# Distance-kernel attention on one core: heads in pairs, strips in two parts, rows read back in two steps

## The reference, cut to what matters

```python
qh, kh, vh = (q @ Wq), (q @ Wk), (q @ Wv)      # each as 16 heads of 8 features
dist = max(q_norm - 2*qk + k_norm, 0)          # per head, 512 x 512
scores = exp(-gamma[h] * SCALE * dist)
scores = where(triu(ones, k=1), scores, 0)
out = (scores @ vh) as (B, S, 128) @ Wo
x = x + out                                    # the input q is layernorm(x)
```

## Time and profile before

| | |
|---|---|
| median of three runs | 2600.57 us |
| the profiled execution, its own time | 2601.68 us |
| its span, first to last instruction | 2599.8 us |
| stage of the change, to the last value matmuls | 0 to 662 us |
| mean granted TensorE clock | 0.879 of 2.4 GHz |

### The profile page before, as it was taken

The page is one execution under the profiler, slowest core; times in us unless marked ns, Lnnn a source line. Parts: engine busy times, 40 slices in busy tenths (PEclk is TensorE's granted clock), DMA queues, the critical chain, the costliest instruction groups (busy, mean ns, idle before and its releaser), DMA issues. The chain is left out here.

```text
span 2599.8 us, 68776 instructions
## 1 busy us (share of the span) xinstructions
PE 2110.7 (81%) x27953; PEld 1528.7 (59%) x27953; DVE 1728.9 (67%) x3790; ACT 1376.9 (53%) x3916; POOL 678.4 (26%) x746
## 2 busy tenths in 40 slices
PE   3787878778689999999839945557999999993896
PEld 1444544444657677777627734455777777762775
DVE  6777787776537777777766676652777777777553
ACT  2666666656257777777613320014777777771332
POOL 4111111110123444444300003311444434431100
PEclk7888898887679999999969967766999999996998
DMA  5323332231000000000000000000000000000002
GB/s 164 108 85 89 95 107 82 88 99 54 1 9 18 19 18 19 19 11 19 19 1 1 2 1 1 0 1 9 19 11 18 19 18 19 19 19 1 1 1 66
DMA packets 65548, 87.64 MB, mean 34 GB/s; under 512 B 6849, under 2 KB 58946, under 8 KB 61766
## 3 DMA queue, kind: packets, MB, share of 16 engines
q1 hardware_dynamic: 64082, 82.81, 11.5%
q10 hardware_dynamic: 1152, 0.43, 0.1%
HBM read 35.42 MB, written 31.03 MB: 26 GB/s over the span
## 5 line engine op out<-in xcount | busy, mean ns | idle before, releaser
L392 ACT ACTIVATE r_pr<-r_dist,k_negc 128x1280 f32<-128x1280 f32 x256 | 333.3, 1330 | 157.6 <-PE r_dist L279 154.9
L1024 POOL TENSOR_TENSOR f2l_pn<-f2l_p,f2l_rs 128x512 f32<-128x512 f32 (+1 forms) x256 | 206.4, 828 | 343.5 <-DVE f2l_rs L951 343.5
L1024 POOL TENSOR_TENSOR f1l_pn<-f1l_p,f1l_rs 128x512 f32<-128x512 f32 (+1 forms) x256 | 206.4, 828 | 343.2 <-DVE f1l_rs L951 343.2
L470 DVE TENSOR_SCALAR r_pr<-r_pr,k_hi,k_lo 128x768 f32<-128x768 f32 x256 | 182.1, 711 | 123.1 <-ACT r_pr L392 123.0
L277 PE MATMUL r_dist<-r_qs,r_ks 54*128 54x384 bf16 (+2 forms) x768 | 165.3, 306 | 103.8 <-DMA r_ks<-rbf_rows 83.1
L474 DVE SCALAR_TENSOR_TENSOR r_pr<-r_pr,k_lo,r_cap 128x512 f32<-128x512 f32 x256 | 225.4, 880 | 0.0
L292 PE MATMUL r_acc<-r_pr,r_vp 128*32 128x128 f32 (+2 forms) x3584 | 195.1, 362 | 31.6 <-ACT r_ot L361 29.7
L901 ACT ACTIVATE f2l_p<-f2l_sm,f2l_nb 128x192 f32<-128x192 f32 x512 | 210.5, 423 | 1.3 <-DVE f2l_nb L944 1.3
L901 ACT ACTIVATE f1l_p<-f1l_sm,f1l_nb 128x192 f32<-128x192 f32 x512 | 210.4, 423 | 1.3 <-DVE f1l_nb L944 1.3
L277 PEld LDWEIGHTS r_dist<-r_qs,r_ks 54*128 54x128 bf16 x768 | 74.6, 103 | 205.5 <-DMA r_ks<-rbf_rows 87.5
L944 DVE TENSOR_REDUCE f1l_nb<-f1l_sm 128x4 f32<-128x768 f32 x128 | 121.8, 952 | 78.0 <-PE f1l_sm L793 77.9
(11 more groups left out here) (415 smaller groups left out, 5364.5 us busy)
## 6 DMA issues: line engine op xcount, KB each, us to landing
rbf_rows<-r_part SPq DMA_DIRECT2D x112, 128.0 KB, 1.8
r_qs<-rbf_rows SPq DMA_DIRECT2D x32, 432.0 KB
r_ks<-rbf_rows SPq DMA_DIRECT2D x32, 432.0 KB
f1l_vs<-f1l_vv SPq DMA_DIRECT2D x32, 256.0 KB, 3.9
f2l_vs<-f2l_vv SPq DMA_DIRECT2D x32, 256.0 KB, 3.9
rbf_rows<-r_part SPq DMA_DIRECT2D x16, 384.0 KB, 2.6
rbf_rows<-r_part SPq DMA_DIRECT2D x16, 256.0 KB, 2.9
out<-k_x SPq DMA_DIRECT2D x4, 1024.0 KB, 9.3
```

The costliest lines, as they stand in the source:

```text
L392: nc.scalar.activation(pr[:, u // 4 % 2, u % 4, :], dist[:, u % 2, 0:RCOLS], ACT.Exp, scale=K["negc"][:, h:h + 1]).then_inc(s_ex, 1)
L470: nc.vector.tensor_scalar(off, off, hi, lo, ALU.min, ALU.max)
L1024: ins = nc.gpsimd.tensor_tensor(pn[:, u % 2, at:at + HU * w].rearrange("p (k c) -> p k c", k=HU), p[:, u % 2, :, cols], r.broadcast_to([P, ...
```

## The change

- **Pairs.** The main loop goes over 8 pairs of heads instead of 16 heads. The matmuls of the two heads of a pair alternate, one in rows 0 to 53 of the array, the other in rows 64 to 117.
- **Two parts.** The diagonal blocks (512 columns) and the others (768 columns) are separate steps on every engine: `diagonal` and `others` on TensorE, two exponentials per head on ScalarE, `masked` and `bounded` on VectorE. Each has semaphores of its own.
- **Values.** Those of a quad are cut into four pieces of 384, 384, 256 and 256 columns, two per pair, and follow three pairs behind. `pr` becomes a ring of five pairs instead of two quads.
- **Projections.** The five uses stand after pairs 0, 1, 2, 3 and 5, `output` after pair 4, the norm of batch b+2 after pair 6. The norms go to 128 partitions of 256 columns by four matmuls in four column groups.
- **Rows in two steps.** SyncE reads the 48 main rows back as soon as they are written, before it waits for the norms; then it writes the norms (4 DMAs) and reads the 6 norm rows (4 DMAs).
- **The start.** x comes in five pieces, the first of one batch; the constants of the later stages are loaded after batch 0's rows; the ones come from a small buffer of their own, and `cap` is bf16. Statistics of the later tokens are interleaved with the first projections.
- Loops are plain Python loops, and the `apart` no-operations and one small copy in `residual` are gone.

The diff, cut to its core; most removed lines are those of the kernel above and are left out, and so is part of the indentation.

```diff
...
+    HALF = S // 2
+    ON = NT * P
+    RING = 5
...
-    npart = sb("npart", [4 * HH, 3, S], BF16)
-    nrest = sb("nrest", [4 * HH, S])
+    npart = sb("npart", [P, 3, HALF], BF16)
+    nrest = sb("nrest", [P, HALF])
+    ones = sb("ones", [3, HH, S], BF16)
...
-    pr = sb("pr", [P, 2, 4, RCOLS])
+    pr = sb("pr", [P, RING, 2, RCOLS])
...
-    cap = sb("cap", [P, RH, P])
+    cap = sb("cap", [P, RH, P], BF16)
...
-    AT = (0, 2, 4, 6, 9)
+    PAIRS = RH // 2
+    AT = {0: 0, 1: 1, 2: 2, 3: 3, 5: 4}
+    OUT_AT = 4
+    NORM_AT = 6
...
-    WRITES = 16 * (sum(len(v) for v in SLOTS) + 2)
+    MAIN = 16 * sum(len(v) for v in SLOTS)
+    SIDE = 16 * 4
     READS = 16 * 4
+    PIECES = (((3, 0),), ((3, 1), (2, 0)), ((2, 1), (1, 0)), ((1, 1), (0, 1)))
...
+        def batch(b, par):
             for o in range(2):
                 sp.wait_ge(s_p3, 3 * b + o + 1)
                 for slot, n, which in SLOTS[o]:
                     src = part[:, o, which, :].unsqueeze(1)
                     if n > 1:
                         src = src.broadcast_to([P, n, S])
                     sp.dma_start(rows_d[o, RD * slot:RD * (slot + n)]
+                                 .rearrange("(k d) e h s -> (d e h) k s", d=RD), src).then_inc(s_wm, 16)
+            sp.wait_ge(s_wm, MAIN * (b + 1))
+            wait(sp, s_dg, PAIRS * (b - 1))
+            wait(sp, s_of, PAIRS * (b - 1))
+            if b == 0:
+                for c in range(HH // 2):
+                    for e in range(2):
+                        for o in range(2):
+                            sp.dma_start(ops[o][64 * e:64 * e + NORMS, par, 2 * c:2 * c + 2],
+                                         rows_d[o, 0:NORMS, e, 2 * c:2 * c + 2]).then_inc(s_early[c], 16)
+            else:
+                for e in range(2):
+                    for o in range(2):
+                        sp.dma_start(ops[o][64 * e:64 * e + NORMS, par],
+                                     rows_d[o, 0:NORMS, e]).then_inc(s_ld[par], 16)
             sp.wait_ge(s_p3, 3 * b + 3)
             for o in range(2):
+                for half in range(2):
+                    at = NORMS + 3 * o
+                    r = 32 * (2 * o + half) + RH * o
+                    sp.dma_start(rows_d[o, at:at + 3, :, :, half * HALF:(half + 1) * HALF]
+                                 .rearrange("k e h s -> (e h) k s"), npart[r:r + RH]).then_inc(s_wn, 16)
+            sp.wait_ge(s_wn, SIDE * (b + 1))
             for e in range(2):
                 for o in range(2):
+                    sp.dma_start(ops[o][64 * e + NORMS:64 * e + ROWS, par],
+                                 rows_d[o, NORMS:ROWS, e]).then_inc(s_ld[par], 16)
+            if b == 0:
+                for dst, src in K["later"]:
+                    sp.dma_start(dst, src).then_inc(s_late, 16)
+                for c in range(HH // 2):
+                    sp.wait_ge(s_early[c], 16 * 4)
+            sp.wait_ge(s_ld[par], loaded(b))
+        for b in range(B):
+            batch(b, b % 2)
...
+                    for half in range(2):
+                        g = 2 * o + half
+                        mm = nc.tensor.matmul(misc[32 * g:32 * g + 32, 0:HALF],
+                                              K["norm_sel"][:, o * 2 * RH:(o + 1) * 2 * RH],
+                                              sq[:, o, half * HALF:(half + 1) * HALF], start=True, stop=True)
             else:
                 for j in range(NT):
                     mm = nc.tensor.matmul(misc[:, j * P:(j + 1) * P], zt[:, j * P:(j + 1) * P], K["wv"][:],
                                           start=True, stop=True)
...
-        def scores(b, par, u, i):
-            n = RH * b + u
...
+        def diagonal(b, par, w):
+            n = PAIRS * b + w
+            if b == 0 and w % 2 == 0:
+                pe.wait_ge(s_early[w // 2], 16 * 4)
+            if w == 0:
+                pe.wait_ge(s_ld[par], loaded(b))
+            wait(pe, s_exd, 2 * n)
+            for t in range(NT):
+                for e in range(2):
+                    rows = slice(64 * e, 64 * e + ROWS)
+                    q = slice(t * P, (t + 1) * P)
+                    mm = nc.tensor.matmul(dist[:, e, RDIAG[t]:RDIAG[t] + P], ops[1][rows, par, w, q],
+                                          ops[0][rows, par, w, q], start=True, stop=True)
+            mm.then_inc(s_dg, 1)
+        def others(b, par, w):
+            n = PAIRS * b + w
+            wait(pe, s_exo, 2 * n)
+            for t in (3, 2, 1):
+                for e in range(2):
+                    rows = slice(64 * e, 64 * e + ROWS)
+                    mm = nc.tensor.matmul(dist[:, e, RREST[t]:RREST[t] + P * t],
+                                          ops[1][rows, par, w, t * P:(t + 1) * P],
+                                          ops[0][rows, par, w, 0:P * t], start=True, stop=True)
+            mm.then_inc(s_of, 1)
+        def values(b, par, q, piece):
+            if piece == 0:
+                pe.wait_ge(s_mv, PAIRS * b + 2 * q + 2)
                 if q == 0:
                     pe.wait_ge(s_me, USES * (b + 1))
                     wait(pe, s_ot, b)
+            for t, on in PIECES[piece]:
+                at, n, q0 = (RDIAG[t], P, P * t) if on else (RREST[t], P * t, 0)
+                for g in range(4):
+                    mm = nc.tensor.matmul(acc[32 * g:32 * g + 32, q0:q0 + n], vp[:, par, t, g, 32 * q:32 * q + 32],
+                                          pr[:, (PAIRS * b + 2 * q + g // 2) % RING, g % 2, at:at + n],
+                                          start=(q == 0 and piece == 0), stop=(q == 3 and piece == 3),
+                                          skip_group_check=True)
+            if piece == 3:
                 mm.then_inc(s_pv, 1)
+        def later_values(b, w, second):
+            k = 2 * w + second - 6
+            if k < 0:
+                b, k = b - 1, k + 2 * PAIRS
+            if b >= 0:
+                values(b, b % 2, k // 4, k % 4)
         def output(b, done):
             pe.wait_ge(s_ot, b + 1)
             wait(pe, s_me, done)
+            wait(pe, s_xa, b)
             for j in range(NT):
                 mm = nc.tensor.matmul(misc[:, j * P:(j + 1) * P], ot[:, j * P:(j + 1) * P], K["wo"][:],
...
+        for b in range(B):
+            for w in range(PAIRS):
+                diagonal(b, b % 2, w)
+                later_values(b, w, 0)
+                others(b, b % 2, w)
+                later_values(b, w, 1)
+                if w == OUT_AT and b:
+                    output(b - 1, USES * (b + 1) + USES - 1 if b < B - 1 else USES * B)
+                if w in AT and b < B - 1:
+                    if AT[w] == USES - 1:
+                        wait(pe, s_xa, b)
+                    use(b + 1, AT[w])
+        for k in range(2 * PAIRS - 6, 2 * PAIRS):
+            values(B - 1, (B - 1) % 2, k // 4, k % 4)
         output(B - 1, USES * B)
     @block.scalar
...
+        def exps(n, e, cols, ready, done):
+            h = heads[2 * (n % PAIRS) + e]
+            act.wait_ge(ready, n + 1)
+            nc.scalar.activation(pr[:, n % RING, e, cols], dist[:, e, cols], ACT.Exp,
+                                 scale=K["negc"][:, h:h + 1]).then_inc(done, 1)
+        for k in range(USES):
+            leave(0, k)
+        roots(REST, ROOTS)
+        nc.scalar.preload_act_table_set("natural_log_exp_and_others")
+        for b in range(B):
+            for w in range(PAIRS):
+                n = PAIRS * b + w
+                wait(act, s_pv, (n - RING) // 2 + 1)
+                for e in range(2):
+                    exps(n, e, slice(0, ON), s_dg, s_exd)
+                for e in range(2):
+                    exps(n, e, slice(ON, RCOLS), s_of, s_exo)
+                if w == 2 and b:
                     leave_values(b - 1)
+                if w in AT and b < B - 1:
+                    leave(b + 1, AT[w])
         leave_values(B - 1)
     @block.vector
     def _(dve):
         link = Chain(dve, s_ini)
...
+        def masked(n):
+            for e in range(2):
+                h = heads[2 * (n % PAIRS) + e]
+                dve.wait_ge(s_exd, 2 * n + e + 1)
+                on = pr[:, n % RING, e, 0:ON].rearrange("p (k c) -> p k c", k=NT)
+                nc.vector.scalar_tensor_tensor(on, on, K["lo"][:, h:h + 1],
+                                               cap[:, h, :].unsqueeze(1).broadcast_to([P, NT, P]), ALU.max, ALU.min)
+        def bounded(n):
+            for e in range(2):
+                lo, hi = (K[k][:, heads[2 * (n % PAIRS) + e]:heads[2 * (n % PAIRS) + e] + 1] for k in ("lo", "hi"))
+                dve.wait_ge(s_exo, 2 * n + e + 1)
+                off = pr[:, n % RING, e, ON:]
+                ins = nc.vector.tensor_scalar(off, off, hi, lo, ALU.min, ALU.max)
+            ins.then_inc(s_mv, 1)
...
+        dve.wait_ge(s_cap, 2)
+        for b in range(B):
+            for w in range(PAIRS):
+                n = PAIRS * b + w
+                masked(n)
+                bounded(n)
```

(73 more changed lines are left out.)

162 lines of the change are left out of this document (51 added, 111 removed).

## The result

The changed kernel takes 2626.41 us, the median of four runs (2623.54 to 2628.57), against 2598.97 before in the same comparison. That is 1.0107 times the time before (95% interval 1.0085 to 1.0128): slower by 1.1%. I had predicted 2524, with a range of 2448 to 2575. The profiled execution took 2626.01 us with a span of 2624.2.

What follows compares the result with a forecast made beforehand. The chain of rows through DRAM bounds each batch: 13.5 + 20.5 = 34.0 us, 4.1 less than now. From 2601.7, 61 for 15 periods, 5 for the last batch and 11 for the start leave 2524.7, median 2524; range 2448 to 2575.

Steps and rivals of the forecast that it cites:

- the keys' first part: Start of each batch's chain, after pair 2: ready 13.5 us into the batch, bounds 11.7 and 14.5.
- VectorE's work is the floor of the batch: Main loop: VectorE's 27.7 us per batch set the floor if the rows are early.
- The last batch: Final batch, which waits for no rows: finer order gains 5 us, bounds 0 and 10.
- the matmuls of a pair overlap: Scores on TensorE: a pair's 2560 columns cost 0.8 us, between 0.55 and 1.07, freeing 2 us per batch.
- I take 6.1: Main 48-row reads from DRAM: all sixteen DMA engines carry them, so transfer takes 6.1 us; 10.8 with nine.
- What follows the reads: Behind the main reads: norm write and wait 1.0 us, issue and landing of the 6-row reads 3.3.
- The landing of the parts: Key parts written to DRAM before the main reads: issues end after 6.9 us, landing costs 1.8.
- The start: Before the first batch: smaller first read of x, no memsets, later constants; 11 us gained, bounds 5 and 16.
- The second: Rival on the main reads: still nine engines' time, 10.8 us, period 38.7, 2594 in all; chance 0.10.
- The third: Rival on TensorE: stays at the lower clock, 46 us per batch, 2706 in all; chance 0.06.
- The first: Rival on the rows: early enough that VectorE decides, 29.2 us per batch, 2452 in all; chance 0.17.
- The fourth: Rival on scores: heads of a pair don't overlap, 2 us more per batch, 2539; counted within the forecast's 0.64.

Runs made afterwards that it cites:

- e8_chunks_54: e4_chunks with all 54 rows in each of the 16 pieces, read after the wait for the norms, without separate 6-row reads: 2426.12 us, 0.9323 of before.
- m2_ports: No computation, only groups of reads of 8 KB rows into varied partitions: four of 64 rows took 12.3 us at partition 0, 8.7 at 32.
- m1_dma: No computation, only the row reads in groups, each awaited: four of 54 rows 13.4 us, of 48 rows 12.5, of 6 rows 5.4.
- e4_chunks: Changed kernel, norm writes before main reads, every batch's 48-row reads in 16 pieces awaited separately, 6-row reads behind the first: 2464.63 us, 0.9472 of before.
- e2_one_read: Changed kernel with norm writes first and, from batch 1 on, one set of four 54-row reads after parts and norms landed: 2576.07 us, 0.9901 of before.

## Why the prediction was wrong

**What held.** That the trip of the rows bounds every batch. That the keys' first part comes at 13.5 us (13.3 here). That VectorE's work is the floor of the batch once rows are early: 27.7 us in my sum, and in the changed kernel 415.44 / 15 = 27.7; the period is 27.9 in `e8_chunks_54` and 27.4 without rows, with VectorE busy 98% of the time in both. The last batch gained 5.7 for 5. The exponentials of two parts cost 714 and 939 ns for 690 and 903. VectorE's two instructions of a head take 0.79 + 0.79 us on average, where they took 0.89 + 0.71 before: together the same. I had put `cap` at nothing; no run has it alone. And the matmuls of a pair overlap: a pair's scores take 0.40 + 0.50 = 0.9 us, for 0.8, where 2560 columns one after the other would be 1.07 at 2.4 GHz:

```profile
L424 ACT ACTIVATE r_pr<-r_dist,k_negc 128x768 f32<-128x768 f32 x206 | 178.1, 939 | 7.8 <-PE r_dist L317 7.7
...
L424 ACT ACTIVATE r_pr<-r_dist,k_negc 128x512 f32<-128x512 f32 x206 | 133.0, 714 | 164.4 <-PE r_dist L307 164.4
```
```profile
297.89 0.40 PE L307 MATMUL r_dist<-r_qs,r_ks 54*128 54x128 bf16 x8
...
298.79 0.50 PE L317 MATMUL r_dist<-r_qs,r_ks 54*128 54x384 bf16 x6
```

**The step that failed** is "I take 6.1". I reasoned from a share of 0.55 that nine engines were the limit, and that sixteen would move 16/9 as much. The share did go to 1.08, and the rate stayed at 148 GB/s: each engine only took longer. I had kept 10.8 for it; a group of four 48-row reads measures 11.9 to 12.5 from issue to landing, against my 1.4 + 6.1 = 7.5. That is 4.7 us a batch, by the mean of the two. The row that I compared the reads with the earlier trace rows was a write from 128 partitions, and what it had more of was partitions, not only engines. The Trainium skill (SBUF — State Buffer, "Door 1: The DMA port swizzle") says that partitions 0 to 63 reach eight of the sixteen SBUF ports and 64 to 127 the other eight, with a partition and the one 32 above it on the same port. I had not weighed it. By that table 48, 54 and 64 rows from partition 0 on all put eight rows on the fullest port, and 32 at 0, 64 at 32 and 48 at 40 put four; `m2_ports` agrees, with 12.0 to 12.9 us for the first three and 6.7 to 8.9 for the others. It is not the whole of it, since the 16 pieces of `m1_dma` go to the same partitions in 10.0 us.

**What follows the reads** I put at 1.0 for the norm rows' write and wait, and 3.3 for the small reads: 4.3. Of the 19.1 us from issue to start, 12.2 for the reads leave 6.9, of which the small reads' issue and landing are 5.6 (5.4 in `m1_dma`). My 2 us for "a small transfer" was that of a write; these reads of 6 rows cost far more. The write itself lands 1.3 us after the reads should have ended (326.19 against 312.70 + 12.2), near my 1.0; from its own issue that is 10.2 us, for 24 KB. That is 2.6 us a batch.

**The landing of the parts** took 3.0 for 1.8, their issue 6.4 for 6.9. The terms give 4.7 + 2.6 + 1.2 - 0.5 - 0.2 = 7.8 us for the batch shown, 41.8 against the predicted 34.0; the mean of all 15 is 6.43 more. 15 x 6.43 = 96.5, the start's 4.1, less 0.7 for the last batch, is 99.9 of the 101.3 us between 2524.7 and 2626.0.

**The start** gained 6.9 for 11. The first transposes begin at 12.34, near my 11. What I missed is the wait for the small reads, which here stand behind all 16 pieces; with them behind the first piece only, `e4_chunks` starts its first scores at 38.69, and without them `e8_chunks_54` at 37.15.

**The rivals.** The second (nine engines' time, 10.8 us) had the time of the reads right, and I gave it 0.10. Its reason was wrong: its sign was to be a share of 0.55, and the share is 1.08. Its 2594 was too low, because the 1.0, 3.3 and 1.8 were mine there too. The third, a low clock that feeds itself, is refuted: the granted clock is 0.84 over the 15 batches with the waits, 0.98 in `e8_chunks_54` and 1.00 without rows. It was a consequence of waiting for rows. The first, rows early, did not come about with reads of this kind; the pieces reached it, with 2465 and 2426 around its 2452. The fourth is refuted by the overlap above. What gates a batch is then not all rows but those of its first four heads.

Not settled: why 16 pieces land sooner than four reads of the same rows, and why reads that alternate between the halves don't run side by side (11.5 and 12.1 us in `m1_dma`), while one read across both halves does.

## What to carry to other kernels

A busy share of the DMA engines is no rate: before a transfer is credited with more engines, look at the bytes per us of one that goes to the same partitions. When a whole batch waits for a transfer, ask first which piece of it the first consumer needs, and wait for that piece; this gave 97 us here on the unchanged kernel and 123 on the changed one, while making the work between two waits faster, with the row transfers of before (`e2_one_read`), gave 0.6 us a batch. Small writes behind long reads in one queue landed here when the reads did (10.2 us after issue, where ahead of them it was 1.7), so splitting a transfer to start a part early puts what comes last in series.

## What the runs showed of the hardware that I had not expected

- Four reads into 48, 54 or 64 partitions from 0 on take the same 12.0 to 12.9 us, at 147 to 197 GB/s in the windows shown; four of 64 rows at partition 32 take 8.7, and 393 GB/s in a window.
- Two reads of 96 rows with the source described as 2 x 48 rows took 32.3 us, at a DMA share of 0.12 and 49 GB/s:

```profile
112.00:113.00 1.00, 0.00 (x0) 0.00 (x0) 1.00 0.12 49
```

- The Trainium skill (DMA: Bandwidth & Descriptors, "Why a DMA increments its semaphore by 16 and not by 1") gives sixteen engines for 48 rows, nine for 54 and, with a slowest dimension of 2, two here. The shares of 1.01, 0.52 and 0.12 agree with each; only the third was slow for want of engines.
- Four reads of 6 rows, 48 KB each, cost 5.4 us.
- 48 rows in 16 reads of 96 KB land in 10.0 us, in four reads of 384 KB in 12.5 and 11.9.
